# Attention scores in float32 on row groups of the array, with short keys made by GpSimd

## What is computed

```python
def _L0_xattn_ref(q, k, v):            # k = v = the context
    qh = q.reshape(b, s, 8, 4, 8).transpose(0, 2, 3, 1, 4)   # 8 key heads of 8 channels, 4 query heads each
    scores = jnp.einsum('bkgsd,bktd->bkgst', qh, kh) * scale
    out = jnp.einsum('bkgst,bktd->bkgsd', softmax(scores), vh)
...
x = x + jnp.tanh(g_xattn[0]) * _L0_xattn_ref(_layernorm(x), ctx, ctx)
x = x + jnp.tanh(g_ffn[0]) * _L0_ffn_ref(_layernorm(x), ...)      # 64 experts, the best 8 of each token
x = x + jnp.tanh(g_xattn[1]) * _L1_xattn_ref(_layernorm(x), ctx, ctx, Wc, bc)   # 4 key heads of 16 channels, 4 query heads each
x = x + jnp.tanh(g_ffn[1]) * _L1_ffn_ref(_layernorm(x), ...)
```

## Time and profile before

| | |
|---|---|
| median of 3 executions | 1713.69 us |
| lowest and highest | 1713.4 and 1714.6 us |
| span of the profiled execution, first to last instruction | 1714.7 us |
| PE, DVE, ACT, POOL busy over the span | 69%, 63%, 46%, 52% |
| mean granted TensorE clock | 0.803 of 2.4 GHz |

### The profile page before, as it was taken

One profiled execution on the slowest core, in us unless ns is written; L12 is line 12 of the kernel. 1 busy time (PEld: TensorE's weight loads), 2 busy tenths in 40 slices (PEclk: granted clock), 3 DMA queues, 4 the chain that ended last, 5 costly groups with the idle time before them and its releaser, 6 DMA issues.

```text
span 1714.7 us, 32329 instructions
## 1 busy us (share of the span) xinstructions
PE 1178.8 (69%) x9122; PEld 778.6 (45%) x9132; DVE 1084.7 (63%) x2699; ACT 783.1 (46%) x1599; POOL 883.5 (52%) x846
## 2 busy tenths in 40 slices
PE   4999998133333299999678777871676777846775
PEld 2566665112221266666555555650454444532243
DVE  5899996666666466666444454442765555747898
ACT  3566665122222166666445454441343333433574
POOL 2343343266666633333377777715888888516100
PEclk9999999555555599999777887785788888878878
DMA  9555554032323599999899999984344434100011
GB/s 209 161 151 154 148 154 135 15 115 104 111 106 110 154 281 308 310 301 304 206 242 237 252 246 248 247 199 101 53 54 55 55 55 55 28 1 1 13 37 49
DMA packets 283470, 247.09 MB, mean 144 GB/s; under 512 B 117584, under 2 KB 270032, under 8 KB 282960
## 3 DMA queue, kind: packets, MB, share of 16 engines
q1 hardware_dynamic: 234192, 169.99, 38.9%
q0 software_dynamic: 49152, 75.53, 20.8%
HBM read 111.93 MB, written 117.77 MB: 134 GB/s over the span
## 4 chain that ended last, share of the span: by engine, by line
DMA 24%; DVE 20%; PE 18%; POOL 16%; issue 13%; SPq 4%; ACT 3%; DVEq 1%; POOLq 0%; ACTq 0%
DMA xs<-V 13%; POOL x L632 11%; DMA arena<-xs 8%; PE bank L1493 4%; DVE arena L1318 3%; DMA xs<-arena,V 2%; PE bank L1369 2%; POOL rs L575 2%; PE bank L1381 2%; DVE arena L971 2%; PE bank L1355 2%; PE bank L1569 2%; PE bank L1370 2%; SPq L518 2%; DVE arena L1316 2%
## 5 line engine op out<-in xcount | busy, mean ns | idle before, releaser
L632 POOL DMA_INDIRECT x<-ys,idx x256 | 404.1, 1578 | 129.2 <-issue 57.6
L650 POOL DMA_INDIRECT xs<-V x192 | 187.1, 974 | 207.7 <-DMA xs<-V 188.5
L1493 PE MATMUL bank<-arena,region 128*128 128x128 f16 x2496 | 253.2, 245 | 1.6 <-ACT arena L834 0.9
L834 ACT COPY arena<-bank 128x640 f16<-128x640 f16 x192 | 132.3, 689 | 190.2 <-PE bank L1569 188.2
L1569 PE MATMUL bank<-arena 128*128 128x128 f16 x1440 | 145.2, 240 | 105.3 <-DMA arena<-xs 101.5
L1381 PE MATMUL bank<-arena 128*72 128x256 f32 (+1 forms) x768 | 212.0, 417 | 0.1
L1493 PEld LDWEIGHTS bank<-arena,region 128*128 (+1 forms) x2496 | 187.0, 111 | 19.2 <-issue 6.2
L1569 PEld LDWEIGHTS bank<-arena 128*128 128x128 f16 x1440 | 97.0, 107 | 113.3 <-DMA arena<-xs 85.4
L573 POOL TENSOR_TENSOR ve<-mv,epsilon 128x1 f32<-128x1 f32 x96 | 39.5, 412 | 202.0 <-DVE mv L912 180.0
L1381 PEld LDWEIGHTS bank<-arena 128*72 128x72 f32 (+1 forms) x768 | 117.2, 158 | 46.4 <-issue 13.5
L982 DVE TENSOR_REDUCE arena<-bank 128x8 f32<-128x512 f32 x192 | 124.1, 675 | 15.5 <-PE bank L1355 14.3
(11 more groups left out here) (204 smaller groups left out, 2557.6 us busy)
## 6 DMA issues: line engine op xcount, KB each, us to landing
ys<-arena SPq DMA_DIRECT2D x96, 512.0 KB
arena<-xs SPq DMA_DIRECT2D x288, 160.0 KB
xs<-idx SPq DMA_DIRECT2D x52, 256.0 KB, 2.4
arena<-in_wpairs SPq DMA_DIRECT2D x32, 256.0 KB, 2.6
arena<-in_wpairs SPq DMA_DIRECT2D x128, 64.0 KB, 2.5
x<-ys,idx POOLq DMA_INDIRECT x256, 6.3
out<-arena SPq DMA_DIRECT2D x16, 256.0 KB, 2.2
xs<-idx SPq DMA_DIRECT2D x52, 64.0 KB, 2.1
```

The costliest lines, as they stand in the source:

```text
L632: pool.indirect_dma_start(tile_x(t), None, ys[t // HT], bass.IndirectOffsetOnAxis(ap=idx[:, t, k:k + 1], axis=0), compute_op=ALU.add).then ...
L650: pool.indirect_dma_start(xs[t // HT], bass.IndirectOffsetOnAxis(ap=at_row[:, t, n % 8:n % 8 + 1], axis=0), ROW[t % NROW], None).then_inc( ...
L834: act.copy(XTP[g % 2][q], tpm[n % 2]).then_inc(R_["xt"], 1)
L1493: mm = pe.matmul(o, lhs(a, w, k), rhs(a, w, k), start=(n == 0), stop=(n == 3 * KT - 1))
```

## The change

- **Queries and keys of `scores` are float32.** KH, KL, KD1, KD2 and the masks are gone. `KDS` holds the float32 keys of eight tiles, block-diagonal as they come from memory: SyncE writes each head's channels to its own rows and columns (`keys`, 8 transfers for 4 tiles in the first layer, 4 in the second), over a buffer that is set to zero once per layer and that has constant rows for the maxima (`own_rows`).
- **`scores` uses row groups.** A head pair takes 32 rows of the array (64 in the second layer), and each of the 4 (2) pairs writes a bank of its own. 8 float32 matmuls of 256 columns per tile in the first layer take the place of 16 float16 ones; 4 take the place of 8 in the second.
- **`maxima` uses 64 x 64 quarters.** It multiplies float16 queries with float16 short keys `K16`, half of the head pairs in each half of the rows: 16 matmuls of 256 columns per tile in the first layer (8 of 512 before), 8 of 128 in the second.
- **`values` uses column groups.** Each head pair has its own 32 (64) output rows and no accumulation: 8 float32 matmuls of 256 columns in the first layer, as before, now with 32 columns of weights; 4 in the second.
- **GpSimd** makes K16, the first thing in its step, from KDS (512 elements per partition in the first layer, 256 in the second), and in the first layer it spreads the values, which ScalarE did. The weights' low parts move one step later.
- **VectorE** loses L971 (two), L1028, L918 and the low keys of the first steps (L904), and in the first layer orders the rest anew.
- **Pipeline.** values now run for tile t-1 in step t, the division for t-2, the second layer's norm for t-3: one step more at the end of each attention. The hardware loop holds eight tiles.
- **SyncE** loads a weight pair in three transfers instead of five. In the experts' stage, ahead of the first `again`, it issues the second layer's `own_rows` (2 transfers) and its first two `keys` (8).

PE in one step of the first attention after the loop, float16 and float32 products by line: before,

One product, K16, is new between the gathers and the roots. The core of the diff:

```diff
-LAST = (NT, NT + 2)
+LAST = (NT + 1, NT + 3)
+NKD = 8
+NXG = 4
...
+            def keys(g, layer):
+                nk, d = LAYERS[layer]
+                if g >= 2:
+                    sp.wait_ge(A[layer]["sc_ready"], 4 * (g - 1) * nk // 2)
+                for k in range(nk):
+                    at = k // 2 * (2 * P // nk) + k % 2 * d
+                    sp.dma_start(KDS[at:at + d, g % 2 * 8:g % 2 * 8 + 8, k % 2 * S:(k % 2 + 1) * S],
+                                 ctxT[k * d:(k + 1) * d, 8 * g * S:8 * (g + 1) * S].rearrange("c (b s) -> c b s", b=8)).then_inc(d_kd[g % 2], 16)
...
-                for e in range(2):
-                    for half in range(2):
-                        sp.dma_start(dst[1][half * I:(half + 1) * I, e, :], wpairs[e * I:(e + 1) * I, bass.ds(n, 1), KT * 2 * P:PW].rearrange("p a w -> p (a w)")).then_inc(done, 16)
+                for half in range(2):
+                    sp.dma_start(dst[1][half * I:(half + 1) * I], wpairs[:, bass.ds(n, 1), KT * 2 * P:PW].rearrange("(e i) a w -> i e (a w)", e=2)).then_inc(done, 16)
...
+                if g == NG:
+                    sp.wait_ge(kd_zero, 2)
+                    own_rows(1)
+                    for t in range(2):
+                        keys(t, 1)
...
+                    if inside(t + 2):
+                        if past(t, 0):
+                            pool.wait_ge(a["mx_ready"], (t + 1) * nmx)
+                        pool.wait_ge(d_kd[(q + 2) % NKD // 4], kd_done(t + 2, (q + 2) % NKD, layer))
+                        stand_alone(pool, side_v)
+                        n = nk // 4
+                        pool.tensor_tensor(K16[j][:, :, 0:hk * S].rearrange("p b (n t) -> p b n t", n=n), KD[(q + 2) % NKD].unsqueeze(2).to_broadcast([P, 2, n, 2 * S]),
+                                           cv(f"part{layer}").unsqueeze(1).unsqueeze(3).to_broadcast([P, 2, n, 2 * S]), ALU.mult).then_inc(a["k16_ready"], 1)
...
-                        pe.matmul(o, KD1[j][:, b, kc], Q1[j][:, :, b * S:(b + 1) * S], start=True, stop=False)
-                        mm = pe.matmul(o, KD2[j][0:w, b, kc], Q2[j][0:w, :, b * S:(b + 1) * S], start=False, stop=True)
...
+                    rp = P // npair
+                    for b in range(2):
+                        for n in range(npair):
+                            rows = slice(n * rp, (n + 1) * rp)
+                            mm = pe.matmul(bank[4 + n][:, b * 256:(b + 1) * 256], KD[q][rows, b, :], Q2[q % 2][rows, :, b * S:(b + 1) * S],
                                            start=True, stop=True)
```

More of the change, by code:

```diff
@@ L173, in sweep @@
     for t in range(-3, 4):
-        step(t, t % 2)
-    with eng.Fori(4, NT - 5, 2) as t:
-        step(t, 0)
-        step(t + 1, 1)
+        step(t, t % NKD)
+    with eng.Fori(4, NT - 2 * NKD + 5, NKD) as t:
+        for q in range(NKD):
+            step(t + q, (4 + q) % NKD)
     for t in range(NT - 4, last + 1):
-        step(t, t % 2)
+        step(t, t % NKD)
 def chunks(eng, body):
@@ L211, in flamingo_block @@
     V = sb("V", [P, B, C])
-    KH = sb("KH", [P, B, S], F16)
-    KL = sb("KL", [P, B, S], F16)
+    KDS = sb("KDS", [P, 2 * NKD, 2 * S])
+    KD = [KDS[:, 2 * n:2 * n + 2, :] for n in range(NKD)]
     gate = sb("gate", [P, 4])
@@ L551, in _ @@
             sp.dma_start(bc, bc_in.rearrange("(a d) -> a d", a=1).to_broadcast([P, H])).then_inc(d_late, 16)
+            for t in range(2, NT // 4):
+                keys(t, 1)
             with sp.Fori(0, NCH) as c:
@@ L1386, in step, with maxima @@
-                def step(t, j):
-                    if inside(t + 1):
-                        pe.wait_ge(a["q_ready"], t + 2)
-                        pe.wait_ge(a["kd_ready"], t + 2)
-                        for u in range(nmx // 2):
-                            maxima(t + 1, 1 - j, u)
+                def maxima(t, j, gp):
+                    if past(t, 1) or gp >= 1:
+                        pe.wait_ge(a["mx_done"], t * nmx + 2 * gp)
+                    stand_alone(pe, side_p)
+                    last = [None, None]
+                    for g in range(2 * gpu):
+                        for b in range(2):
+                            for r in range(2):
+                                rows = slice(r * 64, (r + 1) * 64)
+                                last[r] = pe.matmul(bank[2 + r][b * S:(b + 1) * S, g * hk * S:(g + 1) * hk * S],
+                                                    Q1[j][rows, gp * 2 * gpu + g, b * S:(b + 1) * S], K16[j][rows, b, 0:hk * S],
+                                                    start=True, stop=True)
+                    for mm in last:
+                        mm.then_inc(a["mx_ready"], 1)
@@ new lines, in values @@
+                def values(t, j):
+                    pe.wait_ge(a["vd_ready"], (layer + 1) * (t + 1))
+                    pe.wait_ge(a["ex_ready"], (t + 1) * npair)
+                    if past(t, 1):
+                        pe.wait_ge(a["on_ready"], t)
+                    cg = P // npair
+                    for b in range(2):
+                        for n in range(npair):
+                            mm = pe.matmul(bank[1][n * cg:(n + 1) * cg, b * 256:(b + 1) * 256], VD[j][:, b, n * cg:(n + 1) * cg],
+                                           EX[4 * j + n][:, b * 256:(b + 1) * 256], start=True, stop=True)
+                    mm.then_inc(a["pv_ready"], 1)
@@ L1392, in step @@
+                def step(t, q):
+                    j = q % 2
+                    if inside(t - 2):
+                        pe.wait_ge(a["pvs_ready"], t - 1)
+                        for g in range(G):
+                            mm = pe.transpose(bank[1][:, g * P:(g + 1) * P], PVS[:, g, :], ident)
+                        mm.then_inc(a["ot_ready"], 1)
                     if inside(t):
                         pe.wait_ge(a["q2_ready"], t + 1)
-                        pe.wait_ge(a["kl_ready"], t + 1)
@@ L1408, in step @@
-                    if inside(t):
-                        for u in range(nsc, 2 * nsc):
-                            scores(t, j, u)
+                        scores(t, q)
                     if inside(t + 1):
-                        for u in range(nmx // 2, nmx):
-                            maxima(t + 1, 1 - j, u)
+                        for gp in range(1, nmx // 2):
+                            maxima(t + 1, 1 - j, gp)
                     if inside(t + 2):
```

480 lines of the change are left out of this document (217 added, 263 removed).

## The result

The changed kernel takes 1656.4 us in the median of 4 runs, against 1713.6 us for the kernel before in 4 runs. The ratio is 0.966, with a 95% interval of 0.964 to 0.969. I had forecast 1689. The sign was right and the range held the time, but a gain of 57 us stands where the forecast had 25. In the experiments a ratio is to the kernel before, run on the same chip, and takes the fast runs of both alone.

What follows compares the result with a forecast made beforehand. The prediction took PE, with DVE close behind, to bound the first attention and POOL the second. Its terms -50.8 - 3.2 + 4 + 1 + 6 + 20.2 - 2 = -24.8 us gave 1689 us, range 1652 to 1716.

Steps and rivals of the forecast that it cites:

- The step of the first attention: First attention: step falls from 8.15 to 6.4 us (bounds 5.5 and 7.8), -50.8 us over 29 steps.
- the loads go one after the other and the matmuls hide under them: PE, first attention: weight loads are serial, so 16 records of scores cost 16 x 0.125 = 2.0 us.
- The first rival: First attention: row groups overlap weight loads too, loops fall to 5.6 us, 23 us more gain, 1666 us; chance 0.15.
- The loop through ACT: First attention: scores, second maxima, transposition, two exponents and three copies form the longest loop, 6.3 us.
- SyncE at nothing: First attention: SyncE's transfer issues, 5.4 us per step in the mean, cost nothing while the step is above that.
- POOL's sum: First attention: POOL's work with K16 and the values comes to 4.9 us per step, so it isn't the bound.
- The third rival: First attention: POOL and DVE block each other, step 7.0 us, time 1706 us; chance 0.10.
- Start and low keys: First attention's start: cleared buffers and later code load +4 us (2 to 8); dropped low-key products -3.2 us.
- Experts' stage: First reload of the values: ten more SyncE transfers on the chain of waits, +6 us (0 to 9.6).
- Second attention: Second attention: K16 in POOL's row behind the gathers, 0.72 us in 28 steps, +20.2 us (14 to 28).
- K16 is hidden: Second attention: POOL has waits that K16 fills, -20 us, time 1669 us; chance 0.06.
- Behind the last gather: Second attention's end: steps fall from 6.67 to 5.8 us, one more root costs 3.2 us, together -2 us.

Runs made afterwards that it cites:

- experiments 2 and 3: Changed kernel with first-attention scores over all 128 rows: 1730.8 us, ratio 0.999 to the kernel before; with first-attention values over all 128 columns instead: ratio 0.985.
- experiment 6: Changed kernel with SyncE's fills apart from the keys' turn and half of one POOL low product left out: mean step 5.36 us, short steps 4.83 or 4.84.
- experiments 5 and 11: Changed kernel with SyncE's fills apart from the keys' turn: 1649.9 us; the same plus ACT's second-attention K16 and the ten transfers issued earlier: 1631.4 us.
- experiment 7: Changed kernel with each weight pair issued in five transfers, as in the kernel before: 1669.8 us, ratio 0.976 to the kernel before.
- experiment 8: Changed kernel with K16 of the second attention made by ACT instead of POOL: 1636.4 us, ratio 0.957 to the kernel before.
- experiment 10: Changed kernel with SyncE issuing the second attention's own rows and first keys (ten transfers) while the router works: 1650.9 us, ratio 0.964 to the kernel before.
- experiment 1: Changed kernel plus sets of float32 matmuls while PE idles after the first attention: 57 ns per record for row groups in turn, 148 group after group.

## Why the prediction was wrong

**The bound before** was read rightly: PE set the first attention and POOL the second. Taking PE's side by side work away (experiments 2 and 3) makes PE the bound again.

**The step of the first attention** is the term that failed, 5.66 us in the mean and not 6.4. Over the 25 middle steps that is -62.3 us instead of -43.8. The step of the working that was wrong is "the loads go one after the other and the matmuls hide under them": scores 1.08 us (start to start) instead of 2.0, values 1.0 instead of 1.36. The maxima cost 0.7 instead of 1.36, as my lower bound had it: 43 ns each, where one alone would cost 120, so they overlap too. With three times 0.59 for the transpositions PE's sum is 4.5 us where I had 6.2, and PE no longer sets the step. The first rival (overlap of loads, chance 0.15) was right about the loads. I set it low because "no row has float32 loads side by side". That was true, but the earlier trace rows had matmuls in two column groups side by side, and I used this for the matmul part alone. Its step of 5.6 us and its 1666 us are near the measured ones in part by luck: it had the loops at 5.6, where the loop through PE and ACT is 4.83, and POOL and SyncE made up the rest.

**The loop through ACT** of 6.3 us fell with the scores and maxima in it; the short steps of experiment 6 show that it is at most 4.83.

**SyncE at nothing** was wrong in kind. I compared its mean, 5.4 us, with the step. But its eight keys come together in one turn of four, and in that turn 15 transfers take 8.1 us, more than any step in question. The mean hid this. It costs 2 to 3 us in most of these turns and, with the shorter steps that follow them, 0.3 us of the mean step; experiments 5 and 11 get the greater part back. The price itself was near: 8.1/15 = 0.54 us per transfer against my 0.60. For the same reason the five transfers of before would have cost 0.6 us per step (experiment 7).

**POOL's sum** was 4.9 us and is 5.36: its instructions come to 4.7, but its own gaps of 0.43 and 0.29 us, which I had left out, come on top. "So it isn't the bound" held only for a step of 6.4. The third rival, POOL and DVE blocking each other, did not decide: DVE waits for POOL's roots for 21.3 us in 150, which is how POOL's row sets the ordinary step, but the step never came near its 7.0 us. DVE's sum was near: busy 40.73 of 50 us at a step of 5.66 is 4.6 us, where I had 4.4.

**Start and low keys.** I had +4 and -3.2 to the first sums. In the traces the first sum comes 2.7 us earlier, and the next three steps take 17.96 us instead of 30.41, so together -15.1 where I had -4.5. The low keys were mis-sized: DVE's product of 1.08 us also waits for ACT's cast in most of these steps, 1.03 us at 38.94 and 2.41 here, which I did not add:

```profile
49.99 1.08 DVE L904 TENSOR_TENSOR KL<-region,KH 64x896 f16<-64x896 f32 x1 [2.41 <-ACT KH L694]
```

The first root came at 19.15, 2.4 us later than in the earlier trace rows, where I had 4 (2 to 8). At the end, the last three steps take 12.3 us instead of 16.7.

**Experts' stage.** The row of issues is there as forecast, 5.1 us just before the first reload, though that reload is at 846 us in the trace of before; the one in the earlier trace rows, at 881, is the second. The stage as a whole is 1.5 us longer in the two traces, not 6, but two traces of the same kernel differ by 4.5 us there, and experiment 10 doesn't settle how much of the row is hidden. So the size of my term is not shown.

**Second attention.** The mechanism was right, the term too large: 14.1 us against the kernel before, 17.1 against experiment 8, so 0.5 to 0.6 us per K16 instead of the 0.72 of the earlier trace rows. K16 starts while the last gather is still shown as busy, so its duration is not its price; starts are. The rival "K16 is hidden" (0.06) is refuted by experiment 8.

**Behind the last gather** the sign was wrong: +4.3 instead of -2. Steps fell from 6.67 us to 6.24 and not to 5.8, which gives 2 us with the first one; but the two single steps behind them grew from 5.0 and 4.1 us to 6.2 and 5.3, and the third root behind the code load costs 3.9 us, where I had 3.2:

```profile
1462.77 0.18 POOL L595 TENSOR_TENSOR ve<-mv,epsilon 128x1 f32<-128x1 f32 x1 [6.69 <-issue]
...
1466.35 0.19 POOL L595 TENSOR_TENSOR ve<-mv,epsilon 128x1 f32<-128x1 f32 x1 [2.73 <-DVE mv L931]
...
1470.28 0.19 POOL L595 TENSOR_TENSOR ve<-mv,epsilon 128x1 f32<-128x1 f32 x1 [3.11 <-DVE mv L931]
```

K16 is not the reason: with ACT's K16 this stretch is 67.1 us long, with POOL's 66.6. Why the single steps grew was not tried. The pipeline is one step longer, which fits, but that is only argued.

## What to carry to other kernels

Price matmuls in row or column groups in the order in which they are written: in turn they cost 57 ns per record here, group after group 148. Never set a queue's mean against a step: take the turn in which everything comes together, because the engines wait for that one. When the bound engine gets cheaper by a third, work out the next three in line anew, to the tenth of a microsecond. Here POOL at 5.36 and SyncE at 8.1 in one turn of four took over together, with PE's loop at 4.83 close behind, and a small copy moved from the busy engine to an idle one (experiment 8) gave another 15 us.

## What the hardware showed that I had not expected

The granted clock fell to the lower level, 1.2 GHz, three times in the series of experiment 1, and was at 2.4 GHz between (granted clock third from the right):

```profile
212.20:215.40 3.20, 3.20 (x9) 2.49 (x8) 0.00 (x0) 0.00 (x0) 1.04 (x1) 0.50 0.92 294
215.60:239.40 23.80, 23.80 (x207) 18.68 (x205) 19.23 (x75) 2.12 (x5) 7.37 (x8) 1.00 0.01 2
239.50:246.20 6.70, 6.70 (x48) 5.96 (x48) 0.00 (x0) 0.00 (x0) 0.00 (x0) 0.50 0.00 0
246.30:273.50 27.20, 27.20 (x253) 21.85 (x252) 0.00 (x0) 0.00 (x0) 0.00 (x0) 1.00 0.00 1
273.60:276.90 3.30, 3.30 (x10) 2.59 (x9) 0.00 (x0) 0.00 (x0) 0.00 (x0) 0.50 0.00 0
```

So each of the three long sets of full records (from 211.43, 243.07 and 272.91 us) runs in part at the lower level, 0.80 to 0.82 in its mean, while row groups and column groups with 256 moving columns ran at full clock in all rounds. But the full records need not be the cause. Before the first fall PE had stood idle for 1.43 us, and the second fall came in the sets with 32 moving columns that end the first round, before any full record of the second. Ahead of that fall and of the third PE was busy without a pause. What lowers the clock there was not tried.

And a pause can cost PE more than the pause. After the wait of a long step, in which PE was idle for 1.2 to 2.3 us, the scores of the changed kernel take 2.09 us instead of 1.15 in three steps (56.46, 113.90 and 137.38) and 1.53 and 1.79 in two more. It is not so each time: behind an idle time of 1.25 us, at 158.39, the clock stays at 1.00 and the scores take 1.15. In the stretch around the first of the five the granted clock is 0.79, so part of it ran at the lower level of 1.2 GHz:

```profile
52.00:60.00 8.00, 5.89 (x64) 3.48 (x60) 4.25 (x11) 6.32 (x13) 6.24 (x9) 0.79 0.66 183
```
